# A graph network on one core: the sums of the layer-norm convolutions become a ring over two node pairs

## Chip, core and metric

One core of a Trainium2 chip runs the whole program. The metric is the device time of one execution in microseconds (us). Three executions of the kernel before took 10850.13 us in the median, 10847.68 to 10850.53 us.

## What is computed

Four graph networks follow one another on 128 features, 100000 nodes and 50000 edges sorted by destination; each ends with a layer norm over the features. The change touches two convolutions, the last of the second network ("eve") and the last of the third ("sage"). For sage the reference is (the layer norm of `x + out` follows):

```python
def sage_conv(x, src, dst, W_l, W_r, b, num_nodes):
    agg = segment_mean(x[src], dst, num_nodes)
    return agg @ W_l.T + b + x @ W_r.T
...
h = swish(h)
out = sage_conv(h, src, dst, W2_l, W2_r, b2, n)
```

The eve convolution has the same frame (`x @ wself.T + eve @ weve.T + bias`, then the residual `x` and the layer norm), with a maximum and a minimum over a node's edges in place of the mean, mixed and passed through a relu.

## The kernel before

Each convolution is a phase with a program of its own for each engine. The phases of the two layer-norm convolutions are m5 (eve, second layer) and m7 (sage, second layer); the profile leaves such numbers out and writes `m_`. A phase does two kinds of work. **Edge work**: GpSimd (POOL) gathers the source rows of 1024 edges with eight indirect DMAs of 128 rows each, TensorE (PE), ScalarE (ACT) and VectorE (DVE) turn, scan and multiply them in four halves of 512 edges for each pair of such chunks, and POOL adds the results to the table of sums in HBM with eight more indirect DMAs. **Node work**: 98 chunks of 1024 nodes, taken in 49 pairs, two chunks b = 0 and 1 each. `merged_sweep` writes the order out: in every engine's program one edge unit is followed by the node pairs whose sums are complete, most often two. Each engine runs its program strictly in order, so nothing overtakes a waiting instruction.

What a node pair m does in m5 and m7, engine by engine:

- SP (`load_nodes`) loads y (the input rows), x0 (the residual) and the sums, 512 KB for each chunk, once the tile is free, and then fills the next phase's table of sums with its bias.
- PE turns the y rows (L1190), adds x0 through the identity (L1204) and multiplies (L1208), into four PSUM banks, i = 0 to 3, two for each chunk.
- ACT (`scalar`, `finish_scalar`) copies the turned banks to `nodeT` (L1223), takes the root of the variances (L753), and then finishes the pair before, m - 1: `Norm.apply` (L759) writes `o[b]` from `z[b]` in 16 ACTIVATEs, eight a chunk, and `store_before` issues the two stores of `o`. Ahead of `o[b]` it waits until that tile's last store has landed (`out_free`).
- DVE (`vector`) first turns the roots into scale and shift of pair m - 1 (L745, L748), then adds PSUM bank and sums into `z[b]` (L1775, two halves a chunk), takes eight BN_STATS of 128 features for each chunk (L712), and works out the variances (L724 to L739).

There is one z tile for each b. DVE in pair m writes over the z that ACT in the same turn still reads for pair m - 1, and so waits for it:

```python
dve.wait_ge(ph.finished, 2 * m + b + 1)
```

`finished` counts the chunks that ACT has applied. The output tiles `o` are one for each b too.

Of the kernel before, what the change touches and what calls it, by code (L numbers as in the profile page):

```python
# [24 lines left out]
ALU = mybir.AluOpType  # L25
# [3 lines left out]
P = 128  # L29
D = 128  # L30
T = 8
# [13 lines left out]
class Shapes:  # L45


    def __init__(self, n_nodes, n_edges):
        self.n, self.e = n_nodes, n_edges
        self.node_chunks = -(-n_nodes // CH)  # L50
        self.edge_chunks = -(-n_edges // CH)
        self.edge_tiles = self.edge_chunks * T
        self.edges_padded = self.edge_chunks * CH
        self.node_pairs, self.edge_pairs = self.node_chunks // 2, self.edge_chunks // 2
        self.turns = 2 * (self.edge_pairs - 1)
        assert self.node_chunks % 2 == 0 and self.edge_chunks % 2 == 1 and self.edge_pairs > 2
        self.last_nodes = n_nodes - (self.node_chunks - 1) * CH
        assert self.last_nodes % T == 0 and n_nodes < FAR
        self.last_rows = self.last_nodes // T
# [470 lines left out]
class GatNodes:  # L530
# [92 lines left out]
    def vector_start(self, dve):  # L623
        for b in range(2):
            dve.memset(self.z2[b][:, :, :], 0.0).then_inc(self.z2_done[b], 1)
        dve.wait_ge(self.z2_done[0], 1)
        self.ln2.take(dve, self.z2[0], P, 0)
# [51 lines left out]
    def vector(self, dve, t, pair, past):  # L679
        rows = self.pair_rows(pair)  # L680
        self.last_norm(dve, t, self.pair_rows(past)[1])
        self.add_x(dve, t, rows)
        self.end_norm(dve, t)
        self.first_norm(dve, t, rows)
        self.add_beta(dve, t, rows)
        self.end_first_norm(dve, t)
        self.scale_add(dve, t, rows, 0)
        self.take_second(dve, t, rows)
        self.scale_add(dve, t, rows, 1)
# [312 lines left out]
class Conv(Phase):  # L1002
# [232 lines left out]

    def store_before(self, act, m, out):
        act.wait_ge(self.finished, 2 * m + 2)
        act.sem_inc(self.gate, 1)  # L1240
        if isinstance(m, int):
            self.store_pair(act, m - 1, out)
        else:
            with act.If(0 < m):
                self.store_pair(act, (m - 1).with_bounds(min_val=0), out)
            with act.Else():
                for b in range(2):
                    act.sem_inc(self.stored[b], 16)
# [340 lines left out]
class GcnNodes:  # L1589
# [58 lines left out]
    def finish_scalar(self, act, m):  # L1648
        ph = self.ph
        for b in range(2):  # L1650
            n = ph.sh.rows((m - 1) * 2 + b)
            act.wait_ge(self.acc_done, 2 * m + b + 1)
            ph.out_free(act, m, b)
            act.wait_ge(self.gram_done, 2 * m + 1)
            act.activation(self.y1[b][0:n, :, 0:D], self.acc[b][0:n, :, :], ACT.Copy if self.last else ACT.Relu).then_inc(ph.finished, 1)  # L1655
        ph.store_before(act, m, self.y1)
# [77 lines left out]
class LinearNodes:  # L1734


    def __init__(self, ph, weight, finish):
        self.ph, self.weight, self.finish = ph, weight, finish
        self.z, self.o = ([ph.sb(f"{n}{b}", [P, T, D]) for b in range(2)] for n in ("z", "o"))
        self.z_done = ph.sem("z_done")  # L1740
        if finish == "norm":
            self.ln = Norm(ph, "ln", 2 * T)
        self.grants = [(ph.nodes_turned, 2)] + [(ph.used[n], 2) for n in ph.used] + [(s, 16) for s in ph.stored]

    def tensor_start(self, pe):
        pass
# [5 lines left out]
    def tensor_end(self, pe):  # L1752
        pass

    def vector_start(self, dve):
        for b in range(2):
            dve.memset(self.z[b][:, :, :], 0.0).then_inc(self.z_done, 1)
        if self.finish == "norm":
            dve.wait_ge(self.z_done, 2)
            dve.memset(self.ln.stats[:, :, :], 1.0).then_inc(self.ln.step, 1)  # L1760
            self.ln.solve_var(dve, 0)

    def vector(self, dve, m, scattered):
        ph = self.ph
        norm = self.finish == "norm"
        self.finish_vector(dve, m)
        for i in range(4):
            b = i // 2
            n = ph.sh.rows(m * 2 + b)
            half = slice(H * (i % 2), H * (i % 2) + H)  # L1770
            ph.multiplied_node(dve, m, i)
            if i % 2 == 0:
                ph.have(dve, "sums", m, b)
                dve.wait_ge(ph.finished, 2 * m + b + 1)
            dve.tensor_tensor(self.z[b][0:n, half, :], ph.node_out(i, n), ph.buf["sums"][b][0:n, half, :], ALU.add).then_inc(ph.n_out_read, 1)  # L1775
            if i % 2:
                ph.read_node(dve, m, i)
                dve.sem_inc(ph.used["sums"], 1)
                if norm:
                    ins = self.ln.take(dve, self.z[b], n, b * T)  # L1780
                else:
                    dve.sem_inc(self.z_done, 1)
        if norm:
            ins.then_inc(self.ln.step, 1)
            dve.wait_ge(self.ln.ready, m + 1)
            self.ln.solve_var(dve, m + 1)
# [12 lines left out]
    def finish_scalar(self, act, m):  # L1799
        ph = self.ph  # L1800
        if self.finish == "norm":
            self.ln.take_root(act, m, ph.k["ln_eps"])
            act.wait_ge(self.ln.ready, m + 1)
        for b in range(2):
            n = ph.sh.rows((m - 1) * 2 + b)
            ph.out_free(act, m, b)
            if self.finish == "norm":
                self.ln.apply(act, self.o[b], self.z[b], n, b * T).then_inc(ph.finished, 1)
            else:
                act.wait_ge(self.z_done, 2 * m + b + 1)  # L1810
                act.activation(self.o[b][0:n, :, :], self.z[b][0:n, :, :], ACT.Relu if self.finish == "relu" else ACT.Silu).then_inc(ph.finished, 1)  # L1811
        ph.store_before(act, m, self.o)


def run_conv(nc, ph, edges, nodes):
# [864 lines left out]
```

## Time and profile before

| | us |
|---|---|
| median of three runs | 10850.13 |
| profiled execution | 10843.73 |
| its span, first to last instruction | 10841.9 |
| busy PE, DVE, ACT, POOL | 6744.0, 6202.3, 4581.5, 7208.8 |
| first and last ACTIVATE of L759 (m5 and m7) | 5713.2, 8879.8 |

The page puts the span of one execution next to the busy time of each engine. No engine is busy throughout, and the two phases differ, so the rows below are read phase by phase: m5's node pairs run from about 5713 to 6815 us, m7's from about 7913 to 8886 us. An idle time in brackets is that of the engine ahead of the row, with what ended it; "issue" means that the engine waited for nothing that the profile shows.

### The profile page before, as it was taken

What the parts mean: (1) busy time and instruction counts of PE and PEld (TensorE: products, weight loads), DVE (VectorE), ACT (ScalarE), POOL (GpSimd) and SP (SyncE); (2) the same over time, 40 slices, a digit from 0 to 9 for tenths busy, and PEclk for the clock granted to TensorE, in tenths of its full rate; (3) what the DMA queues carried; (4) which work ended last, traced back from release to release, by engine and by line L of the source; (5) the groups of instructions that cost most, each with busy time, mean ns of one, the idle gap of its engine ahead of it and who ended that gap; (6) DMA issues with size and microseconds to landing.
All of it is one profiled execution on the core that took longest, in us unless ns stands there. A gap on an engine that the chain in (4) does not pass through costs nothing. (4 is left out here: it accounts for less than half of the span.)

```text
span 10841.9 us, 165885 instructions
## 1 busy us (share of the span) xinstructions
PE 6744.0 (62%) x36946; PEld 5118.8 (47%) x36947; DVE 6202.3 (57%) x16059; ACT 4581.5 (42%) x8583; POOL 7208.8 (66%) x7532
## 2 busy tenths in 40 slices
PE   2005766677667669978767888445467656555552
PEld 2004666566656653355545555444455543333331
DVE  5225666566556656544435555333355547888888
ACT  0111222233223325544435555333345545777777
POOL 5736776777677750077767665677677767777772
PEclk9998888788889889988989999777778877777775
DMA  7887887799889978767768777677688863433333
GB/s 190 184 200 240 281 281 250 263 344 319 283 284 337 328 266 283 265 217 258 253 209 281 259 267 260 215 247 251 235 276 313 297 221 98 126 127 126 125 119 105
DMA packets 1864966, 2570.80 MB, mean 237 GB/s; under 512 B 255901, under 2 KB 1369141, under 8 KB 1864662
## 3 DMA queue, kind: packets, MB, share of 16 engines
q1 hardware_dynamic: 1134168, 1627.20, 45.5%
q10 hardware_dynamic: 504726, 564.87, 15.5%
q0 software_dynamic: 225792, 375.94, 10.9%
q14 instruction: 220, 1.80, 0.1%
q8 instruction: 60, 0.98, 0.0%
HBM read 1499.55 MB, written 1129.98 MB: 243 GB/s over the span
## 5 line engine op out<-in xcount | busy, mean ns | idle before, releaser
L1081 POOL DMA_INDIRECT sums_gcn<-m_result,m_idx x1176 | 1166.9, 992 | 430.9 <-issue 349.1
L1190 PE MATMUL m_n_bank<-k_ident,m_in_y 128*128 128x128 f32 x5488 | 848.1, 312 | 891.8 <-DMA m_in_y<-node_rows_c 381.0
L1073 POOL DMA_INDIRECT m_rows<-node_rows_a,m_idx x1176 | 1127.7, 959 | 339.6 <-issue 335.8
L1223 ACT ACTIVATE m_nodeT<-m_n_bank 128x512 f32<-128x512 f32 x980 | 535.6, 597 | 1725.7 <-PE m_n_bank L1190 1723.4
L1775 DVE TENSOR_TENSOR m_z<-m_n_bank,m_in_sums 128x512 f32<-128x512 f32 (+1 forms) x784 | 505.7, 686 | 1306.6 <-ACT m_o L1811 355.0
L1190 PEld LDWEIGHTS m_n_bank<-k_ident,m_in_y 128*128 128x128 f32 x5488 | 719.3, 162 | 983.7 <-issue 791.4
L1081 POOL DMA_INDIRECT sums_eve<-m_result,m_idx x784 | 766.0, 977 | 407.4 <-issue 230.1
L1081 POOL DMA_INDIRECT sums_sage<-m_result,m_idx x784 | 765.9, 977 | 268.4 <-issue 231.4
L1686 DVE SCALAR_TENSOR_TENSOR m_acc<-m_n_bank,m_scales,m_res_b 128x128 f32<-128x128 f32 (+1 forms) x2352 | 634.2, 342 | 487.7 <-PE m_n_bank L1208 421.0
L1073 POOL DMA_INDIRECT m_rows<-node_rows_b,m_idx x784 | 754.4, 962 | 226.4 <-issue 222.1
L1629 PE MATMUL m_gram<-m_y 128*128 128x129 f32 (+1 forms) x4800 | 689.5, 308 | 340.6 <-ACT m_y L1655 339.3
L1629 PEld LDWEIGHTS m_gram<-m_y 128*128 128x128 f32 (+1 forms) x4800 | 652.2, 220 | 374.8 <-ACT m_y L1655 372.9
L1122 PE MATMUL m_e_turn<-k_ident,m_rows 128*128 128x128 f32 x2744 | 512.0, 320 | 499.1 <-DVE m_sums L1585 183.6
L1122 PEld LDWEIGHTS m_e_turn<-k_ident,m_rows 128*128 128x128 f32 x2744 | 391.4, 166 | 637.5 <-DVE m_sums L1585 187.1
L759 ACT ACTIVATE m_o<-m_z,m_ln_shift,m_ln_scale 128x128 f32<-128x128 f32 x1600 | 628.4, 485 | 94.6 <-DMA node_rows_c<-m_o 45.0
L1060 POOL COPY m_idx<-k_edge_idx 128x16 int32 (+1 forms) x350 | 74.6, 215 | 872.5 <-POOLq L106 871.8
L2203 POOL DMA_INDIRECT sums_gat<-g_result,g_idx x392 | 453.3, 1156 | 294.3 <-DVE g_result L2497 179.7
L1208 PE MATMUL m_n_bank<-k_gcn,m_nodeT 128*128 128x128 f32 (+1 forms) x4704 | 589.6, 280 | 0.0
L1132 PE MATMUL m_e_out<-k_gcn,m_sums 128*128 128x128 f32 x2352 | 409.4, 329 | 286.7 <-DVE m_result L1402 286.7
L1931 POOL DMA_INDIRECT degree<-deg_both_tab,k_edge_idx x392 | 456.4, 1164 | 179.0 <-issue 119.2
L1208 PEld LDWEIGHTS m_n_bank<-k_gcn,m_nodeT 128*128 128x128 f32 (+1 forms) x4704 | 567.4, 197 | 0.0
L1132 PEld LDWEIGHTS m_e_out<-k_gcn,m_sums 128*128 128x128 f32 x2352 | 357.3, 232 | 346.4 <-DVE m_result L1402 180.9
(299 smaller groups left out, 17513.2 us busy)
## 6 DMA issues: line engine op xcount, KB each, us to landing
m_in_sums<-sums_gcn SPq DMA_DIRECT2D x291, 512.0 KB
m_in_y<-node_rows_a SPq DMA_DIRECT2D x291, 512.0 KB
sums_gcn<-k_gcn_b SPq DMA_DIRECT2D x194, 512.0 KB
node_rows_a<-m_y ACTq DMA_DIRECT2D x194, 512.0 KB
m_in_x<-in_x_dram SPq DMA_DIRECT2D x194, 512.0 KB
m_in_y<-node_rows_b SPq DMA_DIRECT2D x194, 512.0 KB
sums_eve<-k_eve_b SPq DMA_DIRECT2D x194, 512.0 KB
m_in_sums<-sums_eve SPq DMA_DIRECT2D x194, 512.0 KB
```

Of the source, the lines that this page charges most:

```text
L759: ins = act.activation(out[0:n, j, :], z[0:n, j, :], ACT.Identity, bias=self.shift[copy][0:n, at:at + 1], scale=self.scale[copy][0:n, at:a ...
L1073: pool.indirect_dma_start(self.rows[b][:, t, :], None, self.table[:, :], bass.IndirectOffsetOnAxis(self.idx[s][:, t:t + 1], 0)).then_inc(s ...
L1081: pool.indirect_dma_start(self.node_sums[:, :], bass.IndirectOffsetOnAxis(self.idx[s][:, T + t:T + t + 1], 0), self.result[b][:, t, :], No ...
L1122: mm = pe.transpose(bank[:, n * P:(n + 1) * P], self.rows[b][:, H * (i % 2) + n, 0:D], self.k["ident"][:, :])
L1132: mm = pe.matmul(bank[:, n * D:(n + 1) * D], lhs[:, n * P:(n + 1) * P], weight[:, :], start=True, stop=True)
L1190: mm = pe.transpose(self.n_bank[i][:, t * P:t * P + n], self.buf["y"][i // 2][0:n, H * (i % 2) + t, :], self.k["ident"][0:n, 0:n])
L1208: mm = pe.matmul(self.n_bank[i][0:n, t * D:(t + 1) * D], self.nodeT[:, i, t * P:t * P + n], weight[:, :], start=not add, stop=not add or t ...
L1223: act.activation(out, src, ACT.Copy).then_inc(self.n_turn_read, 1)
L1629: mm = pe.matmul(self.gram[:, 0:D + 1], self.y1[b][0:rows[b], t, 0:D], self.y1[b][0:rows[b], t, :], start=False, stop=False, skip_group_ch ...
L1686: ins = dve.scalar_tensor_tensor(out=self.acc[b][0:n, tt, :], in0=ph.node_out(i, n)[:, t, :], scalar=self.scales[b][0:n, tt:tt + 1], in1=s ...
L1775: dve.tensor_tensor(self.z[b][0:n, half, :], ph.node_out(i, n), ph.buf["sums"][b][0:n, half, :], ALU.add).then_inc(ph.n_out_read, 1)
L1931: pool.indirect_dma_start(self.dram["degree"][:, :], bass.IndirectOffsetOnAxis(k["edge_idx"][:, c, 1, t:t + 1], 0), self.both_tab[:, c * T ...
```

## The change

In the two phases that end with a norm, z becomes one tile `ring` of two slots, each for both chunks of a pair. Pair m uses slot m & 1. Inside the loops m is a register, so the slot's address is worked out at run time. `finished` is granted 2 at the start, so that DVE in pair m waits for ACT's turn m - 1 and no longer for its turn m; `store_before` adds the 2 to what it waits for. The output tiles, and ACT's wait for their stores, are as before. The phases that end with relu or silu keep their z tiles.

```diff
-    def store_before(self, act, m, out):
-        act.wait_ge(self.finished, 2 * m + 2)
+    def store_before(self, act, m, out, granted=0):
+        act.wait_ge(self.finished, 2 * m + 2 + granted)
         act.sem_inc(self.gate, 1)
...
     def __init__(self, ph, weight, finish):
         self.ph, self.weight, self.finish = ph, weight, finish
-        self.z, self.o = ([ph.sb(f"{n}{b}", [P, T, D]) for b in range(2)] for n in ("z", "o"))
         self.z_done = ph.sem("z_done")
         if finish == "norm":
+            self.ring = ph.sb("z", [P, 2, 2 * T, D])
             self.ln = Norm(ph, "ln", 2 * T)
-        self.grants = [(ph.nodes_turned, 2)] + [(ph.used[n], 2) for n in ph.used] + [(s, 16) for s in ph.stored]
+        else:
+            self.z = [ph.sb(f"z{b}", [P, T, D]) for b in range(2)]
+        self.o = [ph.sb(f"o{b}", [P, T, D]) for b in range(2)]
+        self.grants = [(ph.nodes_turned, 2)] + [(ph.used[n], 2) for n in ph.used] + [(s, 16) for s in ph.stored] + ([(ph.finished, 2)] if finish == "norm" else [])
     def tensor_start(self, pe):
...
     def tensor_end(self, pe):
         pass
+    def ring_of(self, m, b):
+        rows = slice(b * T, b * T + T)
+        if isinstance(m, int):
+            return self.ring[:, m % 2, rows, :]
+        return self.ring[:, bass.ds(m & 1, 1), rows, :].rearrange("p o t f -> p (o t) f")
     def vector_start(self, dve):
         for b in range(2):
-            dve.memset(self.z[b][:, :, :], 0.0).then_inc(self.z_done, 1)
+            z = self.ring_of(1, b) if self.finish == "norm" else self.z[b]
+            dve.memset(z[:, :, :], 0.0).then_inc(self.z_done, 1)
         if self.finish == "norm":
...
                 dve.wait_ge(ph.finished, 2 * m + b + 1)
-            dve.tensor_tensor(self.z[b][0:n, half, :], ph.node_out(i, n), ph.buf["sums"][b][0:n, half, :], ALU.add).then_inc(ph.n_out_read, 1)
+                z = self.ring_of(m, b) if norm else self.z[b]
+            dve.tensor_tensor(z[0:n, half, :], ph.node_out(i, n), ph.buf["sums"][b][0:n, half, :], ALU.add).then_inc(ph.n_out_read, 1)
             if i % 2:
...
                 if norm:
-                    ins = self.ln.take(dve, self.z[b], n, b * T)
+                    ins = self.ln.take(dve, z, n, b * T)
                 else:
...
             act.wait_ge(self.ln.ready, m + 1)
+        past = m - 1 if isinstance(m, int) else m + 1
         for b in range(2):
...
             if self.finish == "norm":
-                self.ln.apply(act, self.o[b], self.z[b], n, b * T).then_inc(ph.finished, 1)
+                self.ln.apply(act, self.o[b], self.ring_of(past, b), n, b * T).then_inc(ph.finished, 1)
             else:
...
                 act.activation(self.o[b][0:n, :, :], self.z[b][0:n, :, :], ACT.Relu if self.finish == "relu" else ACT.Silu).then_inc(ph.finished, 1)
-        ph.store_before(act, m, self.o)
+        ph.store_before(act, m, self.o, 2 if self.finish == "norm" else 0)
 def run_conv(nc, ph, edges, nodes):
```

What stands in the engines' programs shows what the run-time address adds. The first place is ACT in the loop over node pairs of m5, at the start of the apply. Rows with - are those of before and rows with + those of the change; ISA stands here for a register instruction that works out an address, REGISTER_ALU for one that works out a value, and a name after "waits" is the semaphore by the name of its first user in the program, here that of the store of `o` for chunk 0 and for chunk 1.

```order
 L753 ACTIVATE m_ln_root<-m_ln_tmp,k_ln_eps 128x16 [waits m0_added]
 L1256 ISA [waits m0_gram_done]
-L759 ACTIVATE m_o<-m_z,m_ln_shift,m_ln_scale 128x128 [waits deg_high_scaled0]
-L759 ACTIVATE m_o<-m_z,m_ln_shift,m_ln_scale 128x128 x7
-L759 ACTIVATE m_o<-m_z,m_ln_shift,m_ln_scale 128x128 [waits deg_high_scaled1]
-L759 ACTIVATE m_o<-m_z,m_ln_shift,m_ln_scale 128x128 x7
+L759 REGISTER_ALU [waits deg_high_scaled0]
+L759 ISA
+L759 ACTIVATE m_o<-m_z,m_ln_shift,m_ln_scale 128x128
+L759 ISA
```

The sixteen ACTIVATEs stay and keep their order; one register instruction now stands ahead of each, two ahead of the first, and the wait for the store has moved from the ACTIVATE to a register instruction.

The second place is DVE in the same loop, at the first add into z and the statistics behind it.

```order
-L1774 ISA [waits deg_stored1]
-L1775 TENSOR_TENSOR m_z<-m_n_bank,m_in_sums 128x512 [waits deg_low_scaled1]
-L1231 REGISTER_ALU
-L1775 TENSOR_TENSOR m_z<-m_n_bank,m_in_sums 128x512 [waits deg_x_in1]
+L1785 ISA [waits deg_stored1]
+L1787 REGISTER_ALU [waits deg_low_scaled1]
+L1787 ISA
+L1787 TENSOR_TENSOR m_z<-m_n_bank,m_in_sums 128x512
+L1231 REGISTER_ALU
+L1787 ISA [waits deg_x_in1]
+L1787 TENSOR_TENSOR m_z<-m_n_bank,m_in_sums 128x512
```

Here, too, the wait (`finished`, by the name `deg_low_scaled1`) has moved onto a register instruction, and each add has one more ahead of it; of the eight BN_STATS that follow for each chunk, six get one too.

## Rows read from the trace of the kernel before

**Rows 1.** The page's groups: count, busy us, mean ns, idle before, releaser.

```profile
L759 ACT ACTIVATE m_o<-m_z,m_ln_shift,m_ln_scale 128x128 f32<-128x128 f32 x1600 | 628.4, 485 | 94.6 <-DMA node_rows_c<-m_o 45.0
```

**Rows 2.** Windows: busy PE, PEld, DVE, ACT, POOL; clock, DMA share, GB/s.

```profile
5740.00:6740.00 1000.00, 819.49 (x3970) 531.24 (x3968) 563.19 (x1427) 575.05 (x1258) 665.16 (x721) 0.93 0.78 268
7940.00:8800.00 860.00, 615.15 (x3476) 494.56 (x3475) 501.22 (x1631) 500.15 (x1015) 659.75 (x716) 0.83 0.89 313
```

**Rows 3.** Waits in m5, 5713 to 6815 us: total us, times, longest.

```profile
DVE m_z L1775 <- ACT m_o L759: 182.1, 51, 5.3
ACT m_o L759 <- DMA node_rows_c<-m_o: 45.0, 28, 2.5
```

**Rows 4.** Timeline of ACT, two node pairs of m5 and what follows.

```profile
6213.08 6.28 ACT L759 ACTIVATE m_o<-m_z,m_ln_shift,m_ln_scale 128x128 f32<-128x128 f32 x16 [0.62 <-DVE m_ln_shift L748]
6219.83 0.99 ACTq L1253 DMA_DIRECT2D node_rows_c<-m_o  x2
6221.47 2.06 ACT L1223 ACTIVATE m_nodeT<-m_n_bank 128x512 f32<-128x512 f32 x4 [2.11 <-PE m_n_bank L1190]
6224.75 6.28 ACT L759 ACTIVATE m_o<-m_z,m_ln_shift,m_ln_scale 128x128 f32<-128x128 f32 x16 [1.02 <-DMA node_rows_c<-m_o]
6232.85 0.69 ACT L1480 ACTIVATE m_mix<-m_pool,k_bconv 128x512 f32<-128x512 f32 x1 [1.82 <-issue]
```

**Rows 5.** Timelines of DVE and PE over the same pairs.

```profile
6216.31 1.29 DVE L1775 TENSOR_TENSOR m_z<-m_n_bank,m_in_sums 128x512 f32<-128x512 f32 x2 [3.35 <-ACT m_o L759]
6219.39 1.29 DVE L1775 TENSOR_TENSOR m_z<-m_n_bank,m_in_sums 128x512 f32<-128x512 f32 x2
6236.52 1.28 DVE L1531 TENSOR_TENSOR_SCAN m_hi<-k_same_run,m_hi,m_pool 128x512 f32<-128x512 f32 x1 [1.67 <-ACT m_pool L1499]
6217.40 1.05 PE L1208 MATMUL m_n_bank<-k_self,m_nodeT 128*128 128x128 f32 x8
6220.14 1.25 PE L1190 MATMUL m_n_bank<-k_ident,m_in_y 128*128 128x128 f32 x8 [0.81 <-DVE m_z L1775]
```

**Rows 6.** Timeline of SP's DMA issues over the same pairs.

```profile
6218.65 2.57 SPq L1166 DMA_DIRECT2D m_in_sums<-sums_eve  x2
6221.33 3.50 SPq L1173 DMA_DIRECT2D sums_sage<-k_sage_b  x2
```

**Rows 7.** Waits in m7, 7940 to 8800 us.

```profile
DVE m_z L1775 <- ACT m_o L759: 139.9, 41, 4.5
POOL sums_sage L1081 <- issue: 103.7, 340, 0.3
POOL m_rows L1073 <- issue: 94.7, 329, 0.3
```

**Rows 8.** Timelines of ACT, PE, DVE and POOL at the end of m7.

```profile
8836.79 6.28 ACT L759 ACTIVATE m_o<-m_z,m_ln_shift,m_ln_scale 128x128 f32<-128x128 f32 x16 [0.62 <-DVE m_ln_shift L748]
8840.88 1.05 PE L1208 MATMUL m_n_bank<-k_sage_r,m_nodeT 128*128 128x128 f32 x8
8843.10 1.29 DVE L1775 TENSOR_TENSOR m_z<-m_n_bank,m_in_sums 128x512 f32<-128x512 f32 x2
8847.17 2.16 DVE L1402 SCALAR_TENSOR_TENSOR m_result<-m_e_out,m_e_scales,k_sage_b 128x128 f32<-128x128 f32 x8
8850.14 0.97 POOL L1081 DMA_INDIRECT sums_sage<-m_result,m_idx  x1 [15.13 <-DVE m_result L1402]
```

**Rows 9.** Register instructions of three lines: ns min/median/max, first and last start.

```profile
L1493 ACTq ALU_OP  x120: 35/35/35, 4775.1 to 6710.4; - x120
L1327 ACTq FUSED_REGOPS  x40: 51/61/77, 1023.0 to 1788.9; - x40
L2083 DVEq FUSED_REGOPS  x96: 76/86/109, 318.4 to 843.1; - x96
```

**Rows 10.** Timelines of ACT and DVE: a wait that ends ahead of a register instruction.

```profile
6200.50 0.66 ACT L1499 ACTIVATE m_pool<-m_pool,k_bpool 128x512 f32<-128x512 f32 x1 [1.10 <-PE m_pool L1435]
6201.28 1.28 DVE L1531 TENSOR_TENSOR_SCAN m_hi<-k_same_run,m_hi,m_pool 128x512 f32<-128x512 f32 x1 [0.86 <-ACT m_pool L1499]
```

## The prediction

> **What bounds the kernel now.** The page comes first, to find the work that the change touches: the 1600 ACTIVATEs of L759 are two phases of 50 turns of 16, and what kept ACT idle ahead of them was mostly the store of `o` [rows 1]. Then the busy time by stretch, since the phases differ [rows 2]. In m7's inner 860 us POOL is busy 659.75 us, and the waits put 103.7 + 94.7 us of its idle time down to "issue" [rows 7]: 858 of 860 us, so POOL runs its indirect DMAs end to end and bounds m7. In m5 POOL is busy only 665 of 1000 us and nobody is full.
>
> The waits of m5 then show what the change aims at: DVE waits 182.1 us for L759 ahead of z, 51 times [rows 3], and in m7 139.9 us [rows 7]. These are idle times of DVE, not yet of the kernel. For that the timelines of one m5 step are read side by side. ACT applies for 6.28 us from 6213.08, ends at 6219.36, issues the store at 6219.83, copies the next four banks from 6221.47 and applies again at 6224.75, released by the store of `o`, not by DVE. It ends at 6231.03, and 1.82 us of issue later begins the edge work with L1480 [rows 4]. DVE's first edge instruction after the pair comes at 6236.52 and has itself waited 1.67 us for ACT [rows 5]. So ACT carries m5 through the node pairs, and DVE's wait lies beside it.
>
> **The change part by part.**
>
> (a) The wait removed, m5. In the first pair DVE started z at 6216.31, 3.35 us after it was free [rows 5]. Without the wait only PE holds it: the last multiply ends at 17.40 + 1.05 = 6218.45, so the last half of z ends 0.69 (one of the pair of adds in 1.29 us is about that) later at 6219.14, where it ended at 19.39 + 1.29 = 6220.68. PE then turns the last two banks without its 0.81 us wait [rows 5], and is through ahead of 6220.5. ACT, however, needs 1.82 us of issue after its apply, as it does before L1480, so it can't copy before 19.36 + 1.82 = 6221.18 instead of 6221.47: 0.29 us earlier. That goes into the wait for the store, which ends it at 6224.75 in any case. After the second pair ACT's order is the same. Gain in m5: 0. The stall goes from DVE ahead of z to DVE ahead of scale and shift (L745), since ACT takes the root only after its apply.
>
> (b) The wait removed, m7. POOL has no idle time to give back in the inner stretch. At the end it has: its last eight scatters wait 15.13 us for the results that DVE writes from 8847.17, behind its node pair [rows 8]. That pair's last adds into z ended at 43.10 + 1.29 = 8844.39, 2.78 us ahead of the results. They would be held by PE's last multiply alone, 40.88 + 1.05 = 8841.93, and end at 8842.62; with the same 2.78 us the results begin at 8845.40, 1.8 us earlier. The apply of 8836.79 plus 6.28 ends at 8843.07 and doesn't hold them. Gain: 1.8 us.
>
> (c) Register instructions on ACT. The wait for the store now ends on a register instruction, and that one (0.035 us) and an address instruction (0.061 us) follow before the first ACTIVATE [rows 9]: 0.1 us. A start behind a register instruction shows the same: ACT's L1499 ends at 6201.16 and DVE's L1531, with a register instruction ahead, starts 0.12 us later [rows 10], where z started 0.04 us after its last ACTIVATE (13.08 + 7 x 0.386 + 0.485 = 6216.27; 0.386 is (6.28 - 0.485)/15) [rows 4, 5]. In m5 that is on the path: 50 x 0.1 = 5.0 us; in m7 it is behind POOL but for the last two turns, 0.2 us. The Trainium skill, Perfetto Trace Analysis, section "DVE / Act Engine Instruction", has the sequencer decode on while an engine instruction waits in a queue of its own; by it a wait on a register instruction gives that decoding away, which speaks against the change, and the rows agree.
>
> (d) The other 15 address instructions a turn. One takes 0.061 us on ACT and 0.086 us on DVE [rows 9], an ACTIVATE starts 0.386 us after the one before, and eight BN_STATS lie between the adds' end at 6217.60 and 6219.39, 0.22 us each [rows 5]. They fit in between: 0. If they did not, 16 x 0.061 x 50 = 49 us in m5; on DVE 12 x 0.086 = 1 us a pair, less than the 3.35 us that it is early.
>
> (e) The store's landing. SP reloads the sums of chunk 1 only when z is read: now some 1.5 us earlier (6219.14 for 6220.68), and so the fill of the next table, from 6221.33 [rows 6] to about 6219.8, when the store goes out at 6219.83. Until now the store began beside one load of the sums. The bounds: landing 1.5 us later in each of the 28 turns that it ends [rows 3], +42 us; or earlier, because the loads of the sums are out of its way, until DVE's 0.62 us [rows 4] end the wait, 45.0 - 28 x 0.62 = 27.6 us, with 28 x 0.29 = 8 us of (a) then free. SP's queue has work throughout in both orders, so I take a small loss, 0.25 us a turn: +7 us. This store took 24.75 - 19.83 = 4.9 us from issue to release.
> The Trainium skill, DMA: Bandwidth & Descriptors, section "Anatomy of one DMA" (of GpSimd's path), has about 2.0 us fixed and bytes over 436 GB/s, for 512 KB an estimate of 3.2 us. By that the store would have landed before the shift was ready, no such wait would exist, and the sum would be 5.2 - 1.8 - 8 = -5 us; the trace disagrees, by 1.7 us, and the sum goes by the row.
>
> Sum: 0 - 1.8 + 5.0 + 0.2 + 0 + 7 = +10.4 us. The profiled execution would take 10843.73 + 10.4 = 10854 us; the median of the runs stands 6.4 us above it, so 10850.13 + 10.4 = **10860 us**. A measurement here can tell about 0.2%, 22 us: this is no change.
>
> **The rivals.**
> - The store's wait and POOL stay the bounds, as summed: 10860 us, its own range 10845 to 10880. Chance 0.68.
> - Faster, the store lands earlier: the DMA engines carry the sums before the store goes out. Both parts of (e) come back, -27.6 - 8 - 1.8 + 5.2 = -32: 10818 us. For it speaks that the wait varies from turn to turn up to 2.5 us; against it that the fill comes forward too. It decides from about 1 us a turn. Chance 0.11.
> - Faster, the waits of DVE are the kernel's: 182.1 us of m5 come back, 10668 us. The Trainium skill (Trainium Kernel Development and Optimization, "Best Practices") advises a second buffer for overlap. Against it stand the release of L759 by the store and the 1.67 us of [rows 5]. Chance 0.03.
> - Slower, the store lands later: the fill now runs beside it from the start, +42 + 5.2 - 1.8 = +45: 10895 us. It decides from about 0.7 us a turn. Chance 0.10.
> - Slower, the address instructions are not hidden: +49 + 5.2 - 1.8 = +52: 10902 us. Against it stand the 0.386 us. Chance 0.08.
>
> **How the numbers follow.** The likeliest gives 10860. The range, 10830 to 10890, takes in the whole first case and about half of what lies between it and the second and fourth (their mechanisms can come in part), leaving some 0.2 out. Faster by over 0.2% (below 10828): 0.08 of the second case and the third, 0.11. Slower (above 10872): the last two, less what of them comes in part, and the upper edge of the first, 0.19. The rest is 0.70.
>
> **What would show it.** In the profile of the changed kernel: DVE's wait for L759 ahead of z gone from both phases, and its wait for the root (L745) longer by about as much; in m5 ACT's wait for the store of `o` as long as before or longer (28 times, 45 us; I expect about 60), the sixteen ACTIVATEs still 6.28 us, and the steps of two pairs and an edge unit of the same length within 0.5 us; in m7 POOL end to end and its last wait below 15.13 us by about 1.8. The prediction is wrong if the apply stretches beyond 6.5 us, if L759's wait for the store falls below 20 us, or if the edge work after a pair starts other than 1.8 us after ACT's apply.

## The result

| | before | changed |
|---|---|---|
| median of 5 runs | 10847.68 us | 10897.74 us |
| lowest to highest | 10828.48 to 10850.53 us | 10893.53 to 10904.89 us |
| profiled execution, and its span | 10843.73 us, 10841.9 us | 10893.53 us, 10891.7 us |

The changed kernel is slower: ratio 1.0052, 95% interval 1.0039 to 1.0065. The forecast was 10860 us, no change, with a range that ended at 10890 us.

Where the time went is seen by phase. From the first memset of z of a phase to that of the next, m4 took 1023.56 us before and 1021.11 after, m5 1187.84 and 1253.97, m6 1025.27 and 1023.96; in m7, from that memset to the start of the last ACTIVATE of L759, 1039.3 and 1032.8. What comes ahead of m4 was 8.2 us shorter in this execution, with unchanged code. So m5 lost 66.1 us, m7 gained 6.5, and the rest is within what two executions differ by (how much that is for m5, an experiment below shows).

The page's group of the applies in the changed kernel (count, busy us, mean ns, idle before, releaser) answers to [rows 1]:

```profile
L759 ACT ACTIVATE m_o<-m_z,m_ln_shift,m_ln_scale 128x128 f32 (+1 forms) x1600 | 626.4, 479 | 158.8 <-DMA node_rows_c<-m_o 93.6
```

The same 1600 instructions, 479 ns each for 485: the ring's run-time addresses did not stretch them. The idle time ahead of them grew from 94.6 to 158.8 us, and the part of m5's store from 45.0 to 93.6 (m7's store, of another tensor, adds 5.1 before and 10.9 after).

The windows of the changed kernel (busy PE, PEld, DVE, ACT, POOL; clock, DMA share, GB/s) answer to [rows 2]:

```profile
5740.00:6740.00 1000.00, 780.51 (x3736) 511.18 (x3736) 535.00 (x1344) 539.89 (x1181) 641.36 (x696) 0.91 0.73 253
7940.00:8800.00 860.00, 605.91 (x3432) 493.17 (x3431) 493.42 (x1593) 484.50 (x988) 660.06 (x718) 0.82 0.85 302
```

Every engine does less in the same 1000 us of m5, and the DMA engines too (253 GB/s for 268): nobody became busier, all wait. In m7 POOL is as full as it was.

The waits in m5, 5713 to 6865 us, of the changed kernel (total us, times, longest) answer to [rows 3]:

```profile
DVE m_ln_scale L745 <- ACT m_ln_root L753: 129.2, 49, 4.5
ACT m_o L759 <- DMA node_rows_c<-m_o: 93.6, 24, 4.7
ACT m_o L759 <- DVE m_ln_shift L748: 19.0, 25, 0.8
```

DVE's wait of 182.1 us for L759 ahead of z is gone, and its wait for the root is longer, 129.2 us for 93.0. But the wait for the store, 1.6 us a time before (45.0 / 28), is 3.9 us a time (93.6 / 24).

Now one step of m5, the timelines of ACT, DVE and SP (start, duration, instruction, idle before), to be laid beside [rows 4 to 6]:

```profile
6226.42 6.27 ACT L759 ACTIVATE m_o<-m_z,m_ln_shift,m_ln_scale 128x128 f32 x16 [0.78 <-DVE m_ln_shift L748]
6233.16 1.00 ACTq L1253 DMA_DIRECT2D node_rows_c<-m_o  x2
6234.75 2.06 ACT L1223 ACTIVATE m_nodeT<-m_n_bank 128x512 f32<-128x512 f32 x4 [2.06 <-issue]
6241.08 6.26 ACT L759 ACTIVATE m_o<-m_z,m_ln_shift,m_ln_scale 128x128 f32 x16 [4.07 <-DMA node_rows_c<-m_o]
...
6226.80 0.69 DVE L1787 TENSOR_TENSOR m_z<-m_n_bank,m_in_sums 128x512 f32 x1 [0.66 <-PE m_n_bank L1208]
6231.78 0.69 DVE L1787 TENSOR_TENSOR m_z<-m_n_bank,m_in_sums 128x512 f32 x1 [0.42 <-PE m_n_bank L1208]
...
6231.83 1.18 SPq L1166 DMA_DIRECT2D m_in_sums<-sums_eve  x2
6233.12 2.85 SPq L1173 DMA_DIRECT2D sums_sage<-k_sage_b  x2
```

Count from the start of the apply. Before, z was added from +3.23 to +7.60, SP issued its two loads of the sums in the stretch from +5.57 to +8.14 and the fill from +8.25; the store went out at +6.75, between the two loads. Now z is added from +0.38 to +6.05 and both loads are out by 6231.83 + 1.18 = 6233.01, at +6.59. The store goes out 0.15 us behind the second of them, at 6233.16, and the fill 0.04 us ahead of it. It is released 7.92 us after its issue, where it took 4.92. From the start of one apply to that of the next the step is 14.66 us, for 11.67.

These are single steps, and the one of before is a quick one. Over all turns of m5 in which the store of chunk 0 released the apply (24 in each kernel), the time from issue to release has a median of 5.8 us before (4.7 to 9.0) and of 7.9 after (7.2 to 8.7), and the steps of two pairs one of 12.6 and 14.7 us. The typical loss is 2.1 us a step, and not 3.0.

The DMA view of the changed kernel from the store's issue to its release, 6233.1 to 6241.1 us (queue: packets, MB, share of 16 engines; q1 is SP's, q10 ACT's, q0 POOL's):

```profile
q1 hardware_dynamic: 644, 1.62, 61.2%
q10 hardware_dynamic: 265, 1.00, 30.7%
q0 software_dynamic: 129, 0.26, 9.2%
```

And of the kernel before, 6219.8 to 6224.8 us:

```profile
q1 hardware_dynamic: 276, 1.00, 50.4%
q10 hardware_dynamic: 229, 0.87, 45.7%
```

While the store is on its way SP's queue now moves 1.62 MB and not 1.00 (in 8.0 us for 5.0, so 0.20 MB a us in both), and the store has 31% of the DMA engines and not 46% (0.125 MB a us for 0.174). Two things can have put the bytes there, the second load of the sums or the fill; the trace alone does not say which, and both came forward.

### The profile page after: what moved, and what is told of

Read it like the earlier page. It is cut to its first block and busy times, and to the rows that moved or that the text cites. A ratio compares the mean times of both kernels' runs of the same rounds, so it can differ in the third digit from the quotient of the medians.

```text
span 10891.7 us, 169151 instructions
## 1 busy us (share of the span) xinstructions
PE 6724.3 (62%) x36946; PEld 5119.2 (47%) x36947; DVE 6201.9 (57%) x16059; ACT 4577.8 (42%) x8583; POOL 7202.4 (66%) x7532
## 3 DMA queue, kind: packets, MB, share of 16 engines
q0 software_dynamic: 225792, 375.94, 10.9%
## 5 line engine op out<-in xcount | busy, mean ns | idle before, releaser
L1787 DVE TENSOR_TENSOR m_z<-m_n_bank,m_in_sums 128x512 f32<-128x512 f32 (+2 forms) x784 | 516.2, 686 | 1165.9 <-DMA m_in_sums<-sums_sage 366.5
L759 ACT ACTIVATE m_o<-m_z,m_ln_shift,m_ln_scale 128x128 f32 (+1 forms) x1600 | 626.4, 479 | 158.8 <-DMA node_rows_c<-m_o 93.6
L1208 PE MATMUL m_n_bank<-k_gcn,m_nodeT 128*128 128x128 f32 (+1 forms) x4704 | 598.4, 282 | 0.0
L1208 PEld LDWEIGHTS m_n_bank<-k_gcn,m_nodeT 128*128 128x128 f32 (+1 forms) x4704 | 576.8, 200 | 0.0
L2208 POOL DMA_INDIRECT g_src_rows<-node_rows_b,g_idx x392 | 437.0, 1115 | 112.8 <-issue 112.5
```

The source lines that it names most:

```text
L759: ins = act.activation(out[0:n, j, :], z[0:n, j, :], ACT.Identity, bias=self.shift[copy][0:n, at:at + 1], scale=self.scale[copy][0:n, at:a ...
L1208: mm = pe.matmul(self.n_bank[i][0:n, t * D:(t + 1) * D], self.nodeT[:, i, t * P:t * P + n], weight[:, :], start=not add, stop=not add or t ...
L1787: dve.tensor_tensor(z[0:n, half, :], ph.node_out(i, n), ph.buf["sums"][b][0:n, half, :], ALU.add).then_inc(ph.n_out_read, 1)
```

## The experiments

The four kernels of a group ran on one chip with the kernel before beside them: its median was 10846.76 us in the first group, 10831.14 in the second, 10847.97 in the third. Ratios, with their 95% intervals, are to these. When the expectations of experiments 5 to 8 were written the before had been measured at about 10847 us, 16 us above that of their group, so there the ratio tells more than the time. "m5" is from its first memset of z to that of m6, in one execution.

**1. The ring without the earlier release.** The ring and its run-time addresses stay; DVE waits for the applies as before.

```diff
-        self.grants = [...] + ([(ph.finished, 2)] if finish == "norm" else [])
+        self.grants = [...]
-        ph.store_before(act, m, self.o, 2 if self.finish == "norm" else 0)
+        ph.store_before(act, m, self.o)
```

> The changed kernel with its ring and run-time addresses, but without the grant of 2, so that DVE waits for ACT's apply of the same turn as before. Store theory (the earlier release of DVE lets SP send the loads of the sums and the fill earlier, into the store's time): the store lands as before, ACT waits some 45 us for it in m5, and only the register instructions remain, 50 turns of m5 at 0.1 to 0.2 us: 10853 to 10858 us against 10848 us. Register theory (the address instructions cost the 50 us): 10898 us, as changed. Third theory (DVE's adds and PE's turns beside the apply slow something down): 10853 to 10858 us too; the next run tells it from the first.

Measured: 10850.17 us, ratio 1.0008 (0.9998 to 1.0017). m5 1185.33 us. Waits in m5 (5713 to 6865), ACT:

```profile
ACT m_o L759 <- DMA node_rows_c<-m_o: 41.8, 28, 2.8
ACT m_o L759 <- DVE m_ln_shift L748: 19.8, 26, 0.8
```

All address instructions of the ring are in this kernel, and it costs nothing that can be measured. What costs is the wait that was removed.

**2. The loads of the sums held until the applies.** The changed kernel, and SP waits for the applies that DVE waited for before.

```diff
+                if name == "sums" and self.hold_loads:
+                    sp.wait_ge(self.finished, 2 * m + b + 1)
+                    sp.sem_inc(self.gate, 1)
```

> The changed kernel, grant and ring included, but SP, ahead of each load of the sums in m5 and m7, waits for the apply that DVE used to wait for, so that loads and fill go out when they did before while DVE is free. Store theory: ACT's wait for the store in m5 falls from 93.6 us back to about 45 us, pair follows pair after 12.8 us again instead of 14.6 us, 10850 to 10858 us. Third theory (DVE or PE beside the apply) and register theory: still about 10898 us.

Measured: 10902.61 us, ratio 1.0050 (1.0036 to 1.0064); the store's wait 93.5 us, 24 times. No change, but the hold was too short to test the idea, as a step of its timeline shows:

```profile
5984.98 6.27 ACT L759 ACTIVATE m_o<-m_z,m_ln_shift,m_ln_scale 128x128 f32 x16 [0.78 <-DVE m_ln_shift L748]
5991.71 0.99 ACTq L1257 DMA_DIRECT2D node_rows_c<-m_o  x2
...
5990.36 1.37 SPq L1170 DMA_DIRECT2D m_in_sums<-sums_eve  x2
```

Both loads are still issued by 5991.73, when the store starts. It restored the wait and not the order, and so is inconclusive on the loads as a cause.

**3. The fill behind the store.** The changed kernel; SP issues the fill only when the stores have landed.

```diff
+            if self.hold_fill:
+                for b in range(2):
+                    sp.wait_ge(self.stored[b], 16 * m + 16)
+                    sp.sem_inc(self.gate, 1)
```

> The changed kernel, but SP, ahead of the fill of the next table in m5 and m7, waits until both stores of the turn have landed. It tells the fill from the loads of the sums. Store theory with the fill as culprit: the store lands earlier than before the change, ACT's wait falls from 93.6 us to DVE's share of about 0.8 us a turn, pair follows pair after about 12 us, 10825 to 10845 us, if the fill does not then hold up y of the next pair. If the loads of the sums are the culprit: little is regained, 10880 to 10898 us. Register theory: 10898 us.

Measured: 10901.19 us, ratio 1.0051 (1.0038 to 1.0065); the store's wait 89.8 us, 25 times. A step:

```profile
6138.92 1.22 SPq L1167 DMA_DIRECT2D m_in_sums<-sums_eve  x2
6149.59 1.30 SPq L1178 DMA_DIRECT2D sums_sage<-k_sage_b  x2
...
6140.25 1.01 ACTq L1258 DMA_DIRECT2D node_rows_c<-m_o  x2
6148.16 6.26 ACT L759 ACTIVATE m_o<-m_z,m_ln_shift,m_ln_scale 128x128 f32 x16 [4.07 <-DMA node_rows_c<-m_o]
```

The fill starts 1.43 us after the store is down, and the store takes 7.91 us as ever, behind two loads of the sums that went out ahead of it. Its share of the DMA engines meanwhile (6140.2 to 6148.2 us) is no larger:

```profile
q1 hardware_dynamic: 391, 1.41, 56.7%
q10 hardware_dynamic: 265, 1.00, 30.5%
```

The fill is cleared; of what came forward the loads are left.

**4. The same hold of the fill in the kernel before.**

> The kernel before (no ring) with the same wait ahead of the fill in m5 and m7. If the fill holds up the store already there: ACT's 45.0 us of waiting in m5 fall to about 17 us, 10815 to 10835 us against 10848 us. If it does not (the store's landing is set by the loads of the sums or by a latency of its own): 10845 to 10860 us.

Measured: 10856.51 us, ratio 1.0013 (1.0004 to 1.0022); m5 1206.79 us, the store's wait 50.4 us. The fill is no burden on the store there either; held back, it costs a little.

**5. Only the second load of the sums, behind the store's issue.** ACT counts up a new semaphore when it has issued both DMAs of the store, and SP waits for it ahead of the load for chunk 1.

```diff
+                if name == "sums" and b in self.hold_sums:    # (1,)
+                    sp.wait_ge(self.store_out, m + 1)
+                    sp.sem_inc(self.gate, 1)
...
+        if self.hold_sums:                                    # end of store_before
+            act.sem_inc(self.store_out, 1)
```

> The changed kernel, with one more wait on SP: the load of the sums of chunk 1 goes out only when ACT has issued both DMAs of the store, as it did before the change (store at +6.8 us from the apply's start, that load at about +7.8). Chunk 0 and the fill stay free. Theory A (the store waits in the DMA engines behind the second load of the sums, which now goes out first): the wait for the store of o ahead of L759 in m5 falls from 93.6 us to about 45, steps of two pairs from 14.6 to 12.8 us, and the time to about 10850 us. Theory B (something else of the earlier release of DVE delays ACT, such as the reads of the ring or the register work): the step stays at 14.4 us or more and the time at 10895 us. I expect A: 10852 us, 10840 to 10870.

Measured: 10836.71 us, ratio 1.0003 (0.9994 to 1.0012); m5 1192.56 us. Waits in m5 (5713 to 6815) and a step:

```profile
ACT m_o L759 <- DMA node_rows_c<-m_o: 47.9, 31, 3.4
...
6210.32 6.27 ACT L759 ACTIVATE m_o<-m_z,m_ln_shift,m_ln_scale 128x128 f32 x16 [0.78 <-DVE m_ln_shift L748]
6217.06 1.00 ACTq L1260 DMA_DIRECT2D node_rows_c<-m_o  x2
...
6215.74 3.04 SPq L1171 DMA_DIRECT2D m_in_sums<-sums_eve  x2
```

The two loads are again spread around the store: the second ends its issue at 6218.78, and the store starts at 6217.06. With DVE's early z and the ring left in, this one order gives back the whole loss. The fill did not stay free, as had been expected: it stands behind this load in SP's program and goes out at 6219.01, after the store. Held back alone it changed nothing (experiment 3), so the load is what counts.

**6. Both loads of the sums behind the store's issue.** The same edit with (0, 1).

> The changed kernel, with both loads of the sums held on SP until ACT has issued the store, so that the store goes out ahead of all of them. Theory A (the order of issue decides, a load of 512 KB ahead of the store costs it about 2 us) expects the store to land earlier than before the change: the wait for it ahead of L759 in m5 under 30 us (45.0 before the change), unless the loads of the sums then come too late for DVE; time 10815 to 10845 us. Theory B (the order doesn't matter, what counts is how much moves between two applies) expects the same wait as with the load of chunk 1 alone held, or the 93 us of the changed kernel.

Measured: 10802.29 us, ratio 0.9974 (0.9963 to 0.9985); m5 1159.72 us. The wait for the store is all but gone (5713 to 6778 us: 4.7 us, 4 times), and DVE's shift starts the applies:

```profile
6190.01 6.27 ACT L759 ACTIVATE m_o<-m_z,m_ln_shift,m_ln_scale 128x128 f32 x16 [0.78 <-DVE m_ln_shift L748]
6196.75 1.00 ACTq L1260 DMA_DIRECT2D node_rows_c<-m_o  x2
6201.45 6.31 ACT L759 ACTIVATE m_o<-m_z,m_ln_shift,m_ln_scale 128x128 f32 x16 [0.79 <-DVE m_ln_shift L748]
```

11.44 us from apply to apply, where the changed kernel had 14.66. Over 6196.7 to 6201.5 us, while the store is under way, SP's queue moves 0.36 MB, for 1.00 before, and the store has over half of the DMA engines:

```profile
q10 hardware_dynamic: 235, 0.90, 54.3%
q1 hardware_dynamic: 103, 0.36, 19.4%
```

**7. The suspected cost added to the kernel before.** One more load of 512 KB from the sums, into a tile that nobody reads, ahead of the store. (DVE's wait and the two tiles of z are kept.)

```diff
+                if name == "sums" and b == 0 and self.extra is not None:
+                    sp.wait_ge(self.extra_in, 16 * m + 16)
+                    sp.dma_start(self.extra[...], node_rows(self.streams[name], c, self.sh)).then_inc(self.extra_in, 16)
```

> The kernel before the change, with the suspected cost added to it: right behind the load of the sums of chunk 0 SP loads the same 512 KB once more into a buffer of its own, ahead of the store of ACT; DVE's waits, z and the applies are as before. In m5 and m7. Theory A (one load of 512 KB more ahead of the store delays it by its own length): the wait for the store of o ahead of L759 in m5 rises from 45 us to 80 or more, steps of two pairs from 12.8 to 14.3 us or more, time 10885 to 10920 us. Theory B (the order doesn't matter): under 0.5 us a turn, time under 10875 us.

Measured: 10904.66 us, ratio 1.0061 (1.0047 to 1.0075); m5 1264.94 us. Waits in m5 (5713 to 6865) and a step:

```profile
ACT m_o L759 <- DMA node_rows_c<-m_o: 108.6, 24, 6.1
...
6190.99 0.99 ACTq L1257 DMA_DIRECT2D node_rows_c<-m_o  x2
6199.08 6.26 ACT L759 ACTIVATE m_o<-m_z,m_ln_shift,m_ln_scale 128x128 f32<-128x128 f32 x16 [4.29 <-DMA node_rows_c<-m_o]
...
6189.75 0.33 SPq L1167 DMA_DIRECT2D m_in_sums<-sums_eve  x1
6190.28 0.33 SPq L1171 DMA_DIRECT2D m_extra<-sums_eve  x1
```

Two loads ahead of the store, and it takes 8.09 us from issue to release. The kernel before is as slow as the changed one with nothing else of the change in it. (It also moves more bytes in all, so its time bears out the mechanism and not the exact price.)

**8. The store issued by SP.** The changed kernel; SP issues the store of pair m - 2 in its own queue, ahead of the sums of pair m, and ACT issues none in m5 and m7.

```diff
+            if name == "sums" and self.sp_stores is not None:
+                self.store_earlier(sp, m)      # in load_nodes
...
+    def store_earlier(self, sp, m):            # for 1 < m
+        sp.wait_ge(self.finished, 2 * m + granted)
+        self.store_pair(sp, m - 2, out)
```

> The changed kernel with the store of o issued by SP, in its own queue ahead of the sums of the next turn (behind y and x0), on the same count of finished applies; ACT issues no store in m5 and m7. The queue of SP then keeps the store ahead of the sums and the fill. Theory A: the wait for the store falls under 30 us in m5, and ACT's 1.8 us from its apply to the next copy shrinks to about 0.3 us: steps of two pairs 11 to 12.3 us, time 10760 to 10830 us. Theory B (the order doesn't matter): the wait stays at 45 us or more; the time then falls only by what ACT saves in issue, at most 50 x 1.5 = 75 us. Against both: SP's wait for the applies stands ahead of its sums, as it did before the change.

Measured: 10776.79 us, ratio 0.9945 (0.9931 to 0.9958); m5 1135.64 us. A step:

```profile
6185.70 6.26 ACT L759 ACTIVATE m_o<-m_z,m_ln_shift,m_ln_scale 128x128 f32 x16 [0.86 <-DVE m_ln_shift L748]
6191.87 2.01 ACT L1226 ACTIVATE m_nodeT<-m_n_bank 128x512 f32<-128x512 f32 x4
6195.80 6.27 ACT L759 ACTIVATE m_o<-m_z,m_ln_shift,m_ln_scale 128x128 f32 x16 [1.26 <-DMA node_rows_c<-m_o]
...
6192.36 1.05 SPq L1270 DMA_DIRECT2D node_rows_c<-m_o  x2
6194.03 0.89 SPq L1169 DMA_DIRECT2D m_in_sums<-sums_eve  x2
```

The copies follow the apply at once (1.82 us of issue lay between them), and the step is 10.10 us. The store needs 3.44 us with none of the sums ahead of it. Its wait is still 36.4 us in m5, since ACT is back sooner to ask for it; I had expected under 30.

**9. Both loads held, in the kernel before.** The edit of 6, without the ring.

> The kernel before the change (DVE's wait for the applies kept, two tiles of z) with both loads of the sums held on SP until ACT has issued the store. If the order of issue alone made the gain seen in the ring kernel with the same hold (0.9974), this kernel gains as much: the wait for the store in m5 under 15 us and 10800 to 10815 us. If the ring is needed too (the sums come back after the store, and DVE without the ring would start z later still), it gains less: 10815 to 10835 us. I expect 10810 us.

Measured: 10811.83 us, ratio 0.9963 (0.9949 to 0.9977); m5 1156.28 us, the store's wait 3.7 us, 3 times.

**10. The store issued by SP, in the kernel before.** The edit of 8, without the ring.

> The kernel before the change with the store issued by SP, ahead of the sums of the next turn, and not by ACT; DVE's wait for the applies and two tiles of z as before. With the ring this gave 0.9945. In it ACT's next copies start sooner after the apply, so that DVE's z, which waits for the applies, may now be late. If the ring matters once the store is out of the way, this kernel is slower than its ring version by 10 us or more (10785 to 10810 us); if not, the same within 10 us. I expect 10790 us.

Measured: 10773.69 us, ratio 0.9931 (0.9918 to 0.9945); m5 1114.68 us. This is the fastest version of all; by the ring version's ratio it would have been 10788 us. ACT's waits ahead of L759 in its m5 (5713 to 6753):

```profile
ACT m_o L759 <- DVE m_ln_shift L748: 28.9, 47, 0.6
ACT m_o L759 <- DMA node_rows_c<-m_o: 5.6, 3, 2.3
```

The intervals of 9 and 6, and of 10 and 8, overlap: with the order put right, in either way, the ring gains nothing that can be measured. In 10 the store is waited for 3 times only, where the ring version waits 25 times; in the steps read, the loads of the sums leave 1.66 us behind the store there and 1.67 in the ring version, so it is not they that make the difference. ACT asks for the store later: its step of two pairs is 11.05 us (6190.14 to 6201.19) for 10.10, since it waits 0.51 us for PE ahead of its copies and 1.11 us for DVE ahead of the root. The ring does shorten this step, then, and m5 is still 21 us longer with it. ACT waits longer in the edge work, 170.1 us for PE ahead of L1497 where it waits 141.6 without the ring; why was not tried.

**11. The output tiles doubled, and not z.** The kernel before with a ring over two pairs for o; ACT waits for the store before ahead of issuing the next one.

```diff
+            ph.o_ring = ph.sb("o", [P, 2, 2 * T, D])
...
-                self.ln.apply(act, self.o[b], self.z[b], n, b * T).then_inc(ph.finished, 1)
+                self.ln.apply(act, ph.slot_of(m - 1 if isinstance(m, int) else m + 1, b), self.z[b], n, b * T).then_inc(ph.finished, 1)
```

> The other pair of tiles doubled, alone: the kernel before the change with two tiles of z and a ring of two node pairs for the output o; ACT waits for the store of the pair before only ahead of issuing the next one. If the store's wait is what carries m5 (45.0 us, 28 times, less the 0.62 us a time that DVE's shift would hold ACT all the same), m5 shrinks by about 28 us and with what the edge work gains the time is 10810 us, 10795 to 10825. If DVE's wait for L759 is as good a bound behind it, the gain is under 10 us.

Measured: 10819.36 us, ratio 0.9976 (0.9965 to 0.9987); m5 1167.71 us, and no wait for the store ahead of L759. So the store's wait did carry m5, and its removal gives 28.6 us by the medians (14 to 38 by the interval), where 45.0 - 28 x 0.62 = 27.6 was worked out.

**12. The ring in m7 alone.**

> The ring and the earlier release of DVE in m7 alone; m5 is the kernel before, with two tiles of z. In m7 POOL is the bound, and the changed kernel's m7 was 6.4 us shorter. I expect m7 shorter by 2 to 8 us, m5 1188 us as before, and a time of 10827 us, 10815 to 10835, by the before of this box of runs at 10831 (that is 0.9985 to 1.0). If the loss of m5 were a loss of both phases, m7 would be no shorter.

Measured: 10853.61 us, ratio 1.0002 (0.9993 to 1.0011). The gain of m7 is below what the times can tell. In the profile m7 took 1034.4 us to its last apply, for 1039.3; with the ring it was 1032.4 to 1034.4 us in this and the profiles of 2, 3, 5 and the changed kernel, and without DVE's earlier release 1037.4 to 1039.3 (1, which has the ring too, 4 and before). With both loads held it was 1035.5 with the ring and without it (6 and 9). The time is outside what I had expected, 10815 to 10835 us, which was set by a before of 10831 us, and the before of this group is 10848. The run also shows how much m5 differs between executions: its code is that of before, and it took 1203.73 us here and 1187.84 there. Differences in m5 of under some 16 us between two profiles say nothing.

## Why the prediction was wrong

**What bounds m5: right.** ACT's chain from apply to store to apply carries the steps of two pairs. Experiment 11 takes away the store's wait alone and the kernel is faster by 28.6 us (10847.97 - 10819.36).

**(a) The wait removed, m5: gain 0, right; where the stall goes, wrong in part.** Experiment 5 has the removed wait with the old order around the store, and its ratio is 1.0003. ACT's 1.82 us of issue stayed (2.06 in the step above). But DVE's 182.1 us did not go to L745 by "about as much": its wait there grew by 36.2 us (93.0 to 129.2). The wait for PE's L1208 ahead of z grew from 5.2 to 78.2, and the wait for ACT ahead of the edge work's L1531 from 109.2 to 217.7.

**(b) m7: right in kind, small in size.** 1.8 us was predicted. POOL's last wait fell from 15.13 us [rows 8] to 11.02, by 4.1, and m7 shortened by some 5 to 6.5 us. The multiplies of the last pair also ran sooner behind the root: the last ended 6.07 us after the root's start before (8841.93 - 8835.86) and 4.54 after (8891.58 - 8887.04), which I had taken as fixed.

**(c) Register instructions: right in kind.** 0.1 us a turn was predicted; an apply that follows DVE's shift now starts 0.78 us later for 0.62, so 0.16 us. Experiment 1 has the same instructions and costs nothing that can be measured.

**(d) The other address instructions: right.** The apply takes 6.27 us for 6.28.

**(e) The store's landing: this step failed.** "SP's queue has work throughout in both orders, so I take a small loss, 0.25 us a turn: +7 us." The wait grew by 93.6 - 45.0 = 48.6 us, from 1.6 to 3.9 us a time, so by 2.3, beyond the upper bound of 1.5 us (42 us in all) as well. The shift in time was read rightly: z ends, and the second load goes out, some 1.5 us earlier (z at +6.05 for +7.60). What was missed is what stood in the 1.5 us. The text says itself that "the store began beside one load of the sums"; the store was issued at +6.75 and the second load between that and +8.14. Moving the load forward by 1.5 us takes it past the store's issue, and the store, of another queue, then has two loads ahead of it for one. The cost is not the shift, it is a step in the number of transfers ahead. The times from issue to release, in the steps shown and as medians over the turns that the store released:

```
ahead of the store           step shown   median   kernel
no load of the sums             3.44 us   3.6 us   store_by_sp
one load of 512 KB              4.92 us   5.8 us   before
two loads                       7.92 us   7.9 us   changed
two loads, fill held back       7.91 us   7.8 us   fill_after_store
two loads, one of them added    8.09 us   8.6 us   before_extra_load
```

By the medians the second load costs the store 2.1 us. The first seems to cost as much, 2.2, but the store of the first row is issued by SP and not by ACT. In experiment 6, where ACT issues it with no load ahead, it had landed when the apply was released, 4.70 us after its issue in the step shown.

The rival "the store lands later" gave 10895 us, and the time is 10897.74. It had the price nearly right, and part of that by luck: it blamed the fill, which experiment 3 clears, and its bound of 1.5 us a turn was for a delay and not for a change of order. Its chance of 0.10 was too low: the one row that told the order of issue on the two queues was in hand.

The Trainium skill, DMA: Bandwidth & Descriptors, section "Anatomy of one DMA", gives an estimate of 3.2 us for this store, and the prediction set it aside for the row of 4.9 us. The page's fit is for GpSimd's path and one DMA alone; the trace comes near it where nothing of the sums is ahead, 3.44 us in the step shown and 3.6 in the median. The row less the page's figure, read as the price of one load ahead, would have given an estimate of 1.7 us a turn for a second load; the medians say 2.1.

**The sum.** The store's wait accounts for 48.6 of m5's 66.1 us; register instructions for 25 x 0.16 = 4.0. The other 13.5 us are within the spread of m5 from one execution to another, so no cause can be named for them. A lower clock granted to PE in m5 (0.91 for 0.93 in the windows) goes with the loss. Whether it adds to it was not tried; the version of experiment 8 had 0.93 in the same window too, as the kernel before, with an m5 52 us shorter. With m7's 6.5 us less, 2.5 and 1.3 in m4 and m6, and the 8.2 ahead of m4, this makes 47.6 of the 49.8 us between the two profiled executions.

What stays open: what in the DMA engines makes a load ahead cost the store 2.1 us, and why SP's queue gets 61% of them and the store 31%. A version with both z and o as rings of two pairs was not tried.

## What to carry to other kernels

When a change lets a transfer start earlier, list what is issued between its old and its new time on every queue, and ask whether it passes something that the critical engine waits for; a shift of 1.5 us cost 2.1 us a step in the median and 3.0 in the step shown, since it changed the order. Removing a wait of 182 us that isn't on the path can remove the thing that kept two queues in a good order; if it goes, write that order down as a wait of its own (experiment 5), or put both transfers into one queue (8 and 10). The tile worth doubling is the one whose release the bounding engine waits for: o gave 0.24%, z cost 0.52% and gave nothing with the order put right. With no tile doubled at all, the order gave 0.37% (9), and the same order with the issue moved off ACT to SP 0.69% (10).

## What the runs showed of the hardware

- The latency of a 512 KB store depends on what the other queue issued just ahead of it: 3.44, 4.92 and 7.92 us in the steps shown, 3.6, 5.8 and 7.9 us in the median, with none (the store issued by SP itself), one and two 512 KB loads ahead. The store was issued 0.15 us behind the loads' issue in the last case, and had 31% of the 16 DMA engines until it was released; with both loads behind it, it had 54%.
- Two DMA issues and a branch on ACT cost 1.8 to 2.1 us between two ACTIVATEs; the same issues from SP leave no gap in the step shown.
- An ACTIVATE behind a wait that ends on a register instruction starts 0.16 us later (0.78 for 0.62), while 15 more such address instructions in a row of 16 ACTIVATEs are hidden (6.27 us for 6.28).
